# Rotary embedding on even and odd tiles, one visit of TensorE moved by a step, and a reordered start, in a fused feed-forward, attention, feed-forward kernel

## The reference, cut to what matters

```python
x = x + 0.5 * ffn(layernorm(x))        # mixture of 8 experts, top 2 by the first token of a sample
x = x + attention(layernorm(x))
x = x + 0.5 * ffn(layernorm(x))

def attention(x):                      # x: (32, 512, 256), 16 heads of 16
    q, k, v = split(x @ Wqkv.T)        # per head
    q = cos * q + rotate_half(q) * sin # rotate_half: (x0, x1, x2, ...) -> (-x1, x0, -x3, ...)
    k = cos * k + rotate_half(k) * sin
    scores = q @ k.T / 4, causal
    return (softmax(scores) @ v) @ Wo.T

def ffn(x):                            # per sample: the two experts of its first token
    h = gelu(x @ W1[e] + b1[e]); return mean over e of (h @ W2[e] + b2[e])
```

## Time and profile before

| what | value |
|---|---|
| median of 3 runs (lowest to highest) | 2364.46 us (2361.73 to 2368.14) |
| the profiled execution, its span | 2364.45 us, 2362.7 us |
| first matmul with W1 in f1 | 43.17 us |
| PE, DVE, ACT, POOL busy | 91%, 81%, 58%, 55% |
| granted TensorE clock, mean | 0.975 |

### The profile page before, as it was taken

How to read it: one execution, slowest core, us unless ns; L and a number is a source line. 1 busy time by engine, 2 the same in 40 slices (tenths; PEclk the granted TensorE clock), 3 DMA queues, 4 the chain that set the end, 5 groups by cost and what they waited for, 6 DMA issues and landing times. The chain is left out here.

```text
span 2362.7 us, 53371 instructions
## 1 busy us (share of the span) xinstructions
PE 2148.2 (91%) x18188; PEld 1164.2 (49%) x18188; DVE 1922.6 (81%) x3964; ACT 1358.8 (58%) x2568; POOL 1289.5 (55%) x1459
## 2 busy tenths in 40 slices
PE   2999999579999999999999999999999986999999
PEld 1666666324444444444444444444444433666666
DVE  4777777469989998998998999899899855777776
ACT  2554555136666676666666667666666663455453
POOL 4666666335545554554554555455455424666664
PEclk9999999679999999999999999999999997999999
DMA  5565666334444454444444445444444413666665
GB/s 173 181 199 186 202 200 203 96 66 92 96 93 91 97 101 92 91 96 92 98 95 91 91 97 100 93 91 96 93 98 96 81 37 122 202 204 200 204 200 166
DMA packets 280382, 295.31 MB, mean 125 GB/s; under 512 B 45776, under 2 KB 263216, under 8 KB 280112
## 3 DMA queue, kind: packets, MB, share of 16 engines
q1 hardware_dynamic: 280112, 291.90, 48.8%
HBM read 140.08 MB, written 83.89 MB: 95 GB/s over the span
## 5 line engine op out<-in xcount | busy, mean ns | idle before, releaser
L868 ACT ACTIVATE at_probs<-at_st_ps 128x512 f32<-128x512 f32 x1280 | 747.5, 603 | 467.0 <-PE at_st_ps L973 459.8
L803 DVE TENSOR_REDUCE at_mx<-at_mx_ps 128x1 f32<-128x512 f32 (+3 forms) x1408 | 838.0, 633 | 140.9 <-PE at_mx_ps L955 140.8
L725 POOL TENSOR_SCALAR_AFFINE_SELECT at_probs<-at_probs 128x512 f32<-128x512 f32 x512 | 320.3, 639 | 675.5 <-ACT at_probs L868 672.0
L973 PE MATMUL at_st_ps<-at_q_stack,at_k_stack 49*128 49x512 f16 (+3 forms) x2048 | 460.2, 302 | 73.7 <-ACT at_probs L868 71.6
L950 PE MATMUL at_mx_ps<-at_k_stack,at_q_stack 48*128 48x512 f16 (+3 forms) x2048 | 493.2, 303 | 21.1 <-DMA at_k_stack<-qk_image 11.4
L475 ACT ACTIVATE f_h<-f_h_ps,f_b1s 128x512 f32<-128x512 f32 x256 | 176.1, 688 | 359.0 <-PE f_h_ps L523 348.3
L973 PEld LDWEIGHTS at_st_ps<-at_q_stack,at_k_stack 49*128 49x128 f16 x2048 | 136.1, 94 | 462.4 <-ACT at_probs L868 339.7
L955 PE MATMUL at_mx_ps<-mask,turn 64*128 64x128 bf16 (+2 forms) x1408 | 342.1, 243 | 0.0
L990 PE MATMUL at_pv_ps<-at_probs,at_v 128*32 128x512 f32 (+3 forms) x4096 | 332.1, 442 | 0.1
L539 PE MATMUL f_y_ps<-f_w2hi,f_hhi 128*128 128x256 f16 x1024 | 279.1, 273 | 0.0
L539 PE MATMUL f_y_ps<-f_w2lo,f_hhi 128*128 128x256 f16 x1024 | 279.1, 273 | 0.0
(11 more groups left out here) (117 smaller groups left out, 3911.9 us busy)
## 6 DMA issues: line engine op xcount, KB each, us to landing
at_q_stack<-qk_image SPq DMA_DIRECT2D x192, 128.0 KB, 4.5
at_k_stack<-qk_image SPq DMA_DIRECT2D x192, 128.0 KB, 4.7
f_x<-in_x SPq DMA_DIRECT2D x32, 512.0 KB, 5.7
f_w1hi<-w_hi SPq DMA_DIRECT2D x128, 128.0 KB, 2.5
f_w1lo<-w_lo SPq DMA_DIRECT2D x128, 128.0 KB, 2.1
f_b2s<-in_b SPq DMA_DIRECT2D x128, 128.0 KB, 3.7
f_w2hi<-w_hi SPq DMA_DIRECT2D x128, 128.0 KB, 4.3
f_w2lo<-w_lo SPq DMA_DIRECT2D x128, 128.0 KB, 4.2
```

The costliest lines, as they stand in the source:

```text
L725: nc.gpsimd.affine_select(out=ap, in_=ap, compare_op=ALU.is_ge, fill=0.0, base=0, pattern=[[0, d] for d in dims] + [[1, P]], channel_multi ...
L803: nc.vector.tensor_reduce(o_ap, i_ap, AX_X, ALU.max).then_inc(max_done, 1)
L868: nc.scalar.activation(probs[:, c, :], st_ps[c % 2][:], ACT.Exp, scale=DH ** -0.5).then_inc(exp_done, 1)
L973: ins = nc.tensor.matmul(bank[:, col:col + T - q0], k_stack[ss.par][rows, j + ha, kt * P:(kt + 1) * P], q_stack[ss.par][rows, j + ha, q0:T ...
```

## The change

Three things are changed.

1. The columns of Wqkv for q and k are permuted on the host: tile 0 holds the even features of q of all heads, tile 1 the odd ones, tiles 2 and 3 the same of k. Even and odd partners then sit in the same partition of two tiles. DVE only multiplies by cos. ACT copies the PSUM tile to `raw` (`rope_raw`), POOL multiplies `raw` by an unsigned sin (`rope_sin`), and when both tiles are there makes two sums (`rope_sums`): even = cos*even - sin*odd, odd = cos*odd + sin*even. In POOL's slot both `rope_sin` stand ahead of masks 1 to 3, both sums behind them. `rope_high` and `rope_low` move to later steps. The image in DRAM is read back with another row pattern, of the same number and size of pieces.
2. `turn_output` and the last of the four projection visits move from behind step 5 to behind step 6; DVE's `normalise_output` moves from 5 to 6, its second `begin_rope` from 6 to 7, and ACT's second `v_copy` from 7 to 8.
3. In f1's start, x of sample 1 is loaded ahead of W2; the routes are copied right behind W2; x of sample 2 and the attention weights are issued behind the first weight loads; the masks are copied in the turn of sample 3. The attention weights are split one sample later.

```diff
-            def rope(n, t):
+            def rope_sin(n, t):
                 idx = 4 * n.b + t
                 pool.wait_ge(rope_in, idx + 1)
...
+                wait(pool, rope_done, 4 * n.b + t // 2 * 2)
+                nc.gpsimd.tensor_tensor(by_sin[t % 2][:], raw[t % 2][:], sin_t[:], ALU.mult).then_inc(sin_done, 1)
+
+            def rope_sums(n, u):
+                pool.wait_ge(sin_done, 4 * n.b + 2 * u + 2)
+                for e, op in ((0, ALU.subtract), (1, ALU.add)):
+
+                    wait(pool, qk_lo, 4 * n.b + 2 * u - 1 + e)
+                    nc.gpsimd.tensor_tensor(rotated[e][:], by_cos[e][:], by_sin[1 - e][:], op).then_inc(rope_done, 1)
...
                 if g < 2 and sample(s + 1):
-                    rope(s + 1, 2 * g)
+                    rope_sin(s + 1, 2 * g)
+                    rope_sin(s + 1, 2 * g + 1)
...
                 if g < 2 and sample(s + 1):
-                    rope(s + 1, 2 * g + 1)
+                    rope_sums(s + 1, g)
...
-                nc.vector.tensor_tensor(by_cos[t % 2][:], x_ps[t % 2][:], cos_t[:], ALU.mult)
-                nc.vector.stream_shuffle(swapped[t % 2][:], x_ps[t % 2][:], [i ^ 1 for i in range(32)]).then_inc(rope_in, 1)
+                nc.vector.tensor_tensor(by_cos[t % 2][:], x_ps[t % 2][:], cos_t[:], ALU.mult).then_inc(cos_done, 1)
...
-                    if g in (1, 2) and sample(s + 1) and n in (0, 3):
-                        rope_low(s + 1, 2 * (g - 1) + (n == 3))
-                    if group(G - 3) and n == 5:
+                    if g in (1, 2) and sample(s + 1) and n in (5, 8):
+                        rope_low(s + 1, 2 * (g - 1) + (n == 8))
+                    if group(G - 3) and n == 6:
                         normalise_output(s, g)
-                    if g < 2 and sample(s + 1) and n in (2, 6):
-                        begin_rope(s + 1, 2 * g + (n == 6))
+                    if g < 2 and sample(s + 1) and n in (2, 7):
+                        begin_rope(s + 1, 2 * g + (n == 7))
...
+            def rope_raw(n, t):
+                idx = 4 * n.b + t
+                act.wait_ge(cos_done, idx + 1)
+
+                wait(act, sin_done, idx - 1)
+                nc.scalar.activation(raw[t % 2][:], x_ps[t % 2][:], ACT.Copy).then_inc(rope_in, 1)
...
-                    if g in (1, 2) and sample(s + 1) and n in (0, 2):
-                        rope_high(s + 1, 2 * (g - 1) + (n == 2))
+                    if g in (1, 2) and sample(s + 1) and n in (4, 6):
+                        rope_high(s + 1, 2 * (g - 1) + (n == 6))
+                    if g < 2 and sample(s + 1) and n in (3, 8):
+                        rope_raw(s + 1, 2 * g + (n == 8))
...
-                    if n == 5 and before:
+                    if n == 6 and before:
                         turn_output(s, g)
-                    if g < 2 and sample(s + 1) and n in (0, 1, 4, 5):
-                        project_qk(s + 1, 2 * g + (n > 3), half=(n in (1, 5)))
+                    if g < 2 and sample(s + 1) and n in (0, 1, 4, 6):
+                        project_qk(s + 1, 2 * g + (n > 3), half=(n in (1, 6)))
```

The start of f1 on SP:

```diff
             load_x(0)
             if built:
-                built.load_ffn(sp)
+                built.load_first(sp)
             load_x(1)
-            load_x(2)
             if built:
-                built.load_attention(sp)
+                built.load_second(sp)
             sp.wait_ge(r_top, 2)
             sp.dma_start(routes[:].rearrange("a (b k) -> a b k", k=TOP_K), top_i[:, 0:TOP_K]).then_inc(routes_loaded, 16)
...
             first = load_first(0)
+            load_x(2)
             if built:
                 sp.wait_ge(built.w2_lo, 2)
             load_second(0, first)
+            if built:
+                built.load_attention(sp)
...
+                if s == 3 and built:
+                    built.copy_masks(sp)
```

46 lines of the change are left out of this document (24 added, 22 removed).

## The result

The changed kernel takes 2431.09 us (median of 4 runs, 2425.63 to 2433.59) against 2363.1 us for the kernel before on the same chip: ratio 1.0295, 95% interval [1.0277, 1.0314]. The forecast was 2370, with a range up to 2393: the likeliest case was a slower kernel, and it is slower, but the time is far outside. The profiled execution has a span of 2431.9 us, 69.2 more than before's 2362.7.

The account below looks back on a forecast made before the run. PE was taken as nearly full in the steady attention phase (1274 of 1350 us), DVE almost as full. 2364.5 - 15 (start) + 20 (0.65 us for each of 31 samples) + 0.5 (filling) = 2370 us, range 2340 to 2393.

Parts of the forecast that it names:

- The start: Start of f1: PE's first product 16.6 us sooner, 1.5 us charged back; -15 us, between -11.5 and -17.
- Slot 0: ACT's first copy to raw delays exponential 4: PE's 0.52 us wait at step 8 becomes 0.95 at step 6, +0.33 us.
- the move softens the copy: Slots 0 and 1: with the transposes left at step 5, step 8 would come at about +4.5 instead of +4.39.
- Slot 1: DVE's two lows delay the turned maxima by 0.1 us, contention adds 0.2: +0.3 us, between +0.1 and +0.55.
- The collision of 0.2 us: Slot 1: a low on DVE meets POOL's multiplications of tiles 2 and 3; charged 0.2 us, bounds 0 and 0.45.
- Slot 2: qk_hi and first v copies between ACT's exponentials 4 and 5: +0.07 us, bounds -0.3 and +0.2.
- Slot 3 and POOL: ACT's output splits leave slot 3 at 0 us; masks have 0.7 us to spare, k some 1.5 us.
- The filling of the pipeline: Filling of the attention pipeline, where POOL bounds the first sample's four tiles either way: +0.5 us.
- The busy times: Steady attention window: DVE some 75 us less busy, ACT some 70 us more.
- (a): Attention slots: ACT's copies hide, a sample stays at 45.37 us, only the start is gained; 2350 us; chance 0.20.
- (b): Attention slots: PE's wait at step 8 goes and nothing replaces it; -0.6 us per sample, 2331 us; chance 0.10.
- (c): Slots 1 and 2: POOL's masks come late, PE waits some 0.4 us before step 3; 2395 us; chance 0.15.

Follow-up runs that it names:

- E1: Kernel before with only the change's prologue (loads and order of the feed-forward stage), attention phase untouched; 2350.6 us, ratio 0.995.
- E4: Changed kernel with turned output, normalised output, second begin_rope and second v copy back at their old steps in all slots; 2409.45 us, ratio 1.0206.
- E2: Kernel before with only the move of turned output, last projection visit, normalised output and second v copy to later steps; 2372.54 us, ratio 1.0056.
- E5: Changed kernel with turned output, normalisation, last projection visit and second v copy back at their old positions in slot 2 alone; 2429.0 us, ratio 1.027.
- E10: Changed kernel with the layer-norm statistics moved from slot 2 to slot 0 behind maximum 1, x loaded in the slot 3 ahead; 2405.56 us, ratio 1.0191.
- E17: Kernel before with the change's prologue, large statistics behind step 9 of slot 3, small ones behind step 5 of slot 0; 2423.91 us, ratio 1.027.
- E12: Changed kernel with slot 2's statistics cut in two: four large ones stay at step 1, seven small ones behind maximum 3; 2387.8 us, ratio 1.0108.
- E3: Kernel before with only ACT's high halves moved to steps 4 and 6 and VectorE's low halves to 5 and 8; 2381.11 us, ratio 1.0089.
- E11: Changed kernel with slot 2's two low halves on VectorE behind maxima 8 and 10 instead of 5 and 8; 2450.69 us, ratio 1.038.
- E15: E9 with the four large statistics one by one in slot 0 and the small ones behind step 4 of slot 1; 2358.22 us, ratio 0.9981.
- E16: E9 with the large statistics behind step 9 of slot 3 and the small ones behind step 5 of slot 0; 2365.6 us, ratio 1.0018.
- E9: E4 with ACT's first copy to raw behind exponential 5 instead of 3 and slot 1's second low behind maximum 10; 2425.71 us, ratio 1.0272.

## Why the prediction was wrong

**The start: right in place, short in what is given back.** The product was forecast at 26.6 us and came at 26.71; attention began 13.8 us sooner, within the bounds. I charged 1.5 us for transfers beside the second sample's weights in f1 and did not look at the second feed-forward stage, where the same reordering costs 4.2 us (E1: 5.5). The term, measured by E1's ratio, is 0.005 x 2363 = 12 us instead of 15, and by its interval anything from 8 to 16.

**Slot 0: right.** +0.30 measured, +0.33 forecast, with each step in its place. What the text said beside it, that the move softens the copy, holds for step 8 (E4: 10.88 us with the move undone), but not for the move as a whole: E2 costs 0.25 us per sample alone, and undoing it makes the changed kernel 0.9% faster (1.0206 against 1.0295).

**Slot 1: the size was too high**, +0.08 against +0.3. The collision of 0.2 us that I charged to a low fell on the other engine: the low began first, at 1067.59, and took its 0.68 us, and POOL's product with sin, begun at 1067.78, took 1.61 us instead of 1.27. In E4, where the low began 0.03 us behind the product, the low paid in full.

**Slot 2: this step failed.** "By the same walk +0.07 us, bounds -0.3 and +0.2" followed ACT alone. It is +1.99 us: 31 x 1.99 = 62 of the 69 us. Three things were in the trace or the order and were not brought together. The statistics stand on VectorE at step 1 of slot 2, with maxima 2 and 3 behind them. POOL's two sums of a pair now stand back to back behind three masks, so tile 2's sum, once in slot 1, falls into slot 2 with tile 3's. And the earlier trace rows said what becomes of a VectorE operation with two SBUF inputs inside a POOL operation. I counted POOL's operations ("as many as before") and not where they now lie, and applied contention only to slot 1. E4 and E5 (the same slot 2 without and with the sums beside the small operations, 10.97 and 12.57 or more), E10 (statistics gone, 10.82) and E17 (collision made in the kernel of before) show the cause, and E12 (small ones elsewhere, 11.63) agrees; E3, E5 and E11 show that moved lows, transposes and v copies do not make slot 2 long by themselves.

The Trainium skill ("SBUF — State Buffer", the section on who interferes with whom) says that a VectorE operation with two SBUF inputs, or a `tensor_scalar` in a two-port mode, stands fully still behind a GpSimd operation that reads SBUF. The trace agrees: L105 took 1.23 us for 0.15 and ended with POOL's sum, L115 in E17 1.13 for 0.17. The size of the operation does not matter for what it pays: L105, on 128 x 4 elements, lost 1.08 us, the low in E4, on 128 x 512, 1.10. So the seven small operations took 2.5 us here, more than the four large ones ahead of them (1.4).

**Slot 3 and POOL: right**, +0.03; no wait for masks appeared, and k came in time, though with some 0.9 us to spare in the middle and none in one sample, where I had 1.5: E11, E15 and E16 ran out of it. The filling of the pipeline cost +1.3 us (3.0 - 1.7), not +0.5.

**The busy times: one right by luck.** "DVE some 75 us less busy" came as 74, but mostly because fewer samples fit into the window; per sample it is 0.45 us instead of some 2.5. "ACT some 70 us more" came as 1 us in the window for the same reason; per sample it is 1.9 us.

**Rivals.** (a) and (b) fell: ACT's copies aren't hidden, and PE's waits for ACT stay (64.1 us). (c), a slower kernel by a collision on POOL's side, had the right kind of mechanism at the wrong place. It named masks and PE; it was sums and VectorE.

What stays open: how 0.81 us of slot 2 divide between the statistics' length and the lows that stand ahead of the normalised output; how much of E12's 1.34 us is the collision and how much the later place alone; and POOL's sums moved off the statistics with all else kept, which wasn't tried. E4 comes nearest to it.

## What to carry to other kernels

Where a change reorders one engine of a pair of which one can stand still behind the other, as VectorE and POOL here, lay both queues side by side slot by slot, and look first for chains of tiny two-operand operations in front of something that TensorE waits for: each can cost a whole operation of the other engine. An engine's busy time says nothing on that: it holds the time in which the engine stands still, and over a fixed window it falls when the kernel gets slower. Compare it per sample. And ask in which slot each operation now falls in time, not only in which order: E4 and E5 have the same order in slot 2 and differ by 1.6 us. Time each part of such a change by itself: the 12 us gained in the prologue were hidden under 78 us lost elsewhere.

## What the runs showed of the hardware

- A stall of PE can cost twice. In E9 PE was busy 3.49 us of 1065 to 1070, and from 1070 to 1075 the granted clock was 0.50, the 1.2 GHz level; slots in which the clock fell took 13.8 to 16.5 us where others of the same kernel, with the same wait but no fall, took 12.6 to 12.8. No wait of PE in that stretch of the kernel was longer than 1.51 us. In E10 the same wait of 1.51 us left the clock at 1.00 in 12 samples and brought it down in 16, at 1.57 us each. In the changed kernel most slots 2 kept a clock of 1.00 throughout, as the one from 1069.53 to 1082.46 did.
- A tiny `tensor_scalar` with one SBUF input stood still behind POOL as the two-input ones did (E17: 1.13 us; L107 in the changed kernel: 0.56 inside a mask).
- Which of the two engines pays goes by which begins first: in the changed kernel a low that began 0.19 us ahead of POOL's product took its usual 0.68 us and the product 1.61 instead of 1.27; in E4 a low that began 0.03 us behind the product took 1.78 and the product 1.27.
- Shortening slots that PE fills made the next one worse: E9 has the shortest slots 0 and 1 of all and is 2.7% slower than before.
